# Attention layer of a four-layer graph network: halves of x prepared one step earlier, projections and aggregation in another order, a shorter softmax chain

## The reference

```python
def _L1_gnn_ref(x, adj_matrix, W_qk, W_v):
    qk = jnp.einsum('bnd,ed->bne', x, W_qk)
    q, k = jnp.split(qk, 2, axis=-1)
    v = jnp.einsum('bnd,ed->bne', x, W_v)
    inv_scale = 1.0 / ATT_DIM ** 0.5
    scores = jnp.einsum('bnd,bmd->bnm', q, k) * inv_scale
    w = jnp.sum(scores * adj_matrix, axis=-1, keepdims=True)
    w = jax.nn.softmax(w, axis=1)
    return w * v
...
x = _layernorm(x + _L0_gnn_ref(x, adj, ...), axis=-1)
x = _layernorm(x + _L1_gnn_ref(x, adj, L1_gnn_W_qk, L1_gnn_W_v), axis=-1)
x = _layernorm(x + _L2_gnn_ref(x, adj, ...), axis=-1)
x = _layernorm(x + _L3_gnn_ref(x, adj, ...), axis=-1)
```

## Time and profile before

| | |
|---|---|
| median of 3 runs | 685.64 us (684.79 to 686.12) |
| the profiled execution | 688.34 us, of which the span of its trace is 686.5 us |
| granted PE clock over the span | 0.982 |
| PE busy | 630.0 us (92%), DVE 563.2 us (82%), ACT 528.3 us (77%), POOL 372.0 us (54%) |
| layer 1 on PE | from 284.4 us to 390.6 us of the span |

### The profile page before, as it was taken

How to read it: one execution, slowest core, us unless ns; L and a number is a source line. 1 busy time by engine, 2 the same in 40 slices (tenths; PEclk the granted TensorE clock), 3 DMA queues, 4 the chain that set the end, 5 groups by cost and what they waited for, 6 DMA issues and landing times.

```text
span 686.5 us, 15919 instructions
## 1 busy us (share of the span) xinstructions
PE 630.0 (92%) x5014; PEld 454.4 (66%) x5014; DVE 563.2 (82%) x1744; ACT 528.3 (77%) x1191; POOL 372.0 (54%) x448
## 2 busy tenths in 40 slices
PE   5899999999999999789999789999999997999993
PEld 4577777777777776556655456676767564778782
DVE  3899988888888886768887859898989897578886
ACT  4667888777777887668887776787778785799995
POOL 1335556665555555756665524444444343798883
PEclk9999999999999999999999899999999998999998
DMA  9682439364554322566665523645444443487883
GB/s 278 180 210 52 91 70 224 80 160 94 142 120 97 63 32 47 107 134 130 139 136 111 93 63 77 100 90 105 91 95 94 98 88 63 79 179 182 175 189 124
DMA packets 176771, 80.35 MB, mean 117 GB/s; under 512 B 122416, under 2 KB 174128, under 8 KB 176688
## 3 DMA queue, kind: packets, MB, share of 16 engines
q1 hardware_dynamic: 166512, 70.54, 43.7%
q0 software_dynamic: 8448, 8.39, 8.4%
q10 hardware_dynamic: 1728, 0.40, 0.3%
HBM read 28.97 MB, written 8.39 MB: 54 GB/s over the span
## 4 chain that ended last, share of the span: by engine, by line
PE 31%; DMA 8%; DVE 7%; POOL 7%; issue 4%; ACT 3%; SPq 0%; ACTq 0%; POOLq 0%; DVEq 0%
PE banks L86 10%; PE banks L88 9%; PE banks L87 9%; DMA xT_lo<-x_halves 6%; POOL x_halves L1130 3%; DMA l_TT_lo<-l_T_lo 2%; DVE l_st L1044 2%; POOL l_rstd L1069 2%; DVE l_pre L1321 1%; POOL l_U L1976 1%; PE banks L1569 1%; PE banks L1847 1%; ACT x_resident L1078 1%; POOL l_T_lo L1773 1%; PE banks L1234 1%
## 5 line engine op out<-in xcount | busy, mean ns | idle before, releaser
L1078 ACT ACTIVATE x_resident<-l_pre,l_nmr,l_rstd 128x256 f32<-128x256 f32 x256 | 142.1, 606 | 10.6 <-POOL l_nmr L1072 9.9
L973 POOL TENSOR_TENSOR hq<-hq 128x512 f32<-128x512 f32 x48 | 69.4, 1446 | 94.1 <-ACT hq L690 91.8
L1130 POOL TENSOR_TENSOR x_halves<-x_resident,x_halves 128x1024 f16<-128x1024 f32 x46 | 98.1, 2132 | 28.5 <-DVE l_pre L1321 24.4
L1044 DVE BATCH_NORM_STATS2 l_st<-l_pre 128x6 f32<-128x256 f32 x256 | 92.2, 412 | 0.0
L86 PE MATMUL banks<-Wk_lo,xT_hi 128*128 128x258 f16 (+1 forms) x256 | 84.3, 329 | 1.2 <-DVE l_hr L1691 0.6
L87 PE MATMUL banks<-Wk_hi,xT_lo 128*128 128x258 f16 (+1 forms) x256 | 84.2, 329 | 0.0
L88 PE MATMUL banks<-Wk_hi,xT_hi 128*128 128x258 f16 (+1 forms) x256 | 84.1, 329 | 0.0
L1069 POOL TENSOR_TENSOR l_rstd<-l_veps,minus_half 128x4 f32<-128x4 f32 x64 | 70.1, 1095 | 18.5 <-DVE l_veps L1058 14.2
L86 PE MATMUL banks<-W2T_lo,h_hi 128*128 128x257 f16 x256 | 70.3, 274 | 5.2 <-ACT zf L702 3.4
L88 PE MATMUL banks<-W2T_hi,h_hi 128*128 128x257 f16 x256 | 70.1, 274 | 0.0
L87 PE MATMUL banks<-W2T_hi,h_lo 128*128 128x257 f16 x256 | 70.1, 274 | 0.0
(11 more groups left out here) (202 smaller groups left out, 1911.0 us busy)
## 6 DMA issues: line engine op xcount, KB each, us to landing
adj<-in_adj SPq DMA_DIRECT2D x32, 256.0 KB, 3.7
x_halves<-in_x SPq DMA_DIRECT2D x16, 512.0 KB, 4.4
x_resident<-b_half SPq DMA_DIRECT2D x8, 1024.0 KB, 8.1
x_resident<-in_x POOLq DMA_DIRECT2D x16, 512.0 KB, 6.0
out<-x_resident SPq DMA_DIRECT2D x15, 512.0 KB, 3.3
l_adjT<-adjT_resident SPq DMA_DIRECT2D x16, 256.0 KB, 2.6
x_resident<-in_L_gnn_W SPq DMA_DIRECT2D x2, 512.0 KB, 5.4
x_resident<-in_L_gnn_Wk SPq DMA_DIRECT2D x1, 768.0 KB, 9.6
```

What stands on the lines that cost most here:

```text
L973: pool.tensor_tensor(hq[:, 0, :], hq[:, 0, :], hq[:, h, :], ALU.add).then_inc(hqs_ok, 1)
L1044: dve.bn_stats(L.st[p][:, j, :], L.pre[p][:, j, :]).then_inc(L.st_ok, 1)
L1078: act.activation(K.x[:, gcols(g, j)], L.pre[p][:, j, :], ACT.Identity, bias=L.nmr[p][:, j:j + 1], scale=L.rstd[p][:, j:j + 1]).then_inc(L. ...
L1130: pool.tensor_tensor(F.xs[p][1], x_group(K, g), F.xs[p][0], ALU.subtract).then_inc(F.x_lo, 1)
```

## The change

In layer 1:

- The halves of x for group g+3, not g+2, are made and transposed in step g of ACT, POOL and SP; ACT makes the high half ahead of all four `norm_apply`, not behind the first.
- `aggregate` reads the resident adjacency itself; the copies `l_adjT` and their 16 DMAs are gone.
- PE's step is now project(g-1, 3), weight_columns(g-2), project(g, 0), aggregate(g-1), project(g, 1), the first half of project(g, 2), score_rows(g-1), the second half of project(g, 2).
- The factor -SC goes into the product with q, so that DVE's minimum of the rows is at once the bias of the exponential; the separate negation is gone.
- `residual` takes the weights as its per-partition scalar straight from PSUM; their copy to SBUF is gone.
- DVE's order: two rows of statistics, the minimum, the other two rows, the division (softmax), and then the variance.
- SP's seam between layers 0 and 1 is 'noonnn', not 'nononn'.

```diff
-SEAMS_SP = ('nononn', 'oono', 'onooonon')
+SEAMS_SP = ('noonnn', 'oono', 'onooonon')
...
-            if halves_due(F, g + 2):
-                transpose_x(F, sp, g + 2, p, (qkv_ps, GP))
-            if has(2):
-                stage_adj(g + 2, p)
+            if halves_due(F, g + 3):
+                transpose_x(F, sp, g + 3, 1 - p, (qkv_ps, GP))
...
         def aggregate(g, p):
-            pe.wait_ge(a_in[p], 8 * (g - p) + 16)
             pe.wait_ge(qkv_sb, upto(g, GP, GP))
...
-                m = pe.matmul(b_as[p][:, j * (QK + 1):(j + 1) * (QK + 1)], ast[p][:, j * N:(j + 1) * N],
+                m = pe.matmul(b_as[p][:, j * (QK + 1):(j + 1) * (QK + 1)],
+                              K.at[:, g * C + j * N:g * C + (j + 1) * N],
                               vqk[p][:, j, D + QK:D + 2 * QK + 1], start=True, stop=True)
...
                 weight_columns(g - 2, p)
+            if has(0):
+                project(g, p, 0)
             if has(-1):
                 aggregate(g - 1, q)
             if has(0):
-                project(g, p, 0)
                 project(g, p, 1)
+                project(g, p, 2, 0)
             if has(-1):
                 score_rows(g - 1, q)
             if has(0):
-                project(g, p, 2)
+                project(g, p, 2, 1)
...
-            act.activation(wexp[p][:], b_as[p][0:GP, rows], ACT.Exp, bias=wneg[p][:], scale=SC,
+            act.activation(wexp[p][:], b_as[p][0:GP, rows], ACT.Exp, bias=wmin[p][:], scale=-1.0,
                            accum_out=wsum[p][:]).then_inc(wexp_ok, 1)
...
+            if halves_due(F, g + 3):
+                high_half(g + 3, q)
             if has(-2):
                 norm_apply(K, L, act, g - 2, p, 0)
-            if halves_due(F, g + 2):
-                high_half(g + 2, p)
-            if has(-2):
                 norm_apply(K, L, act, g - 2, p, 1)
...
-            dve.tensor_copy(wgt[p][:], b_as[p][:, cols]).then_inc(wgt_ok, 1)
...
-            dve.scalar_tensor_tensor(L.pre[p][:, j, :], vqk[p][:, j, 0:D], wgt[p][:, j:j + 1],
+            dve.scalar_tensor_tensor(L.pre[p][:, j, :], vqk[p][:, j, 0:D], b_as[p][:, cols.start + j:cols.start + j + 1],
                                      K.x[:, gcols(g, j)], ALU.mult, ALU.add).then_inc(L.pre_ok, 1)
...
-            dve.tensor_tensor(qa[:], ak[:, :, 0:QK], vqk[p][:, :, D:D + QK], ALU.mult).then_inc(qa_ok, 1)
+            dve.scalar_tensor_tensor(qa[:], ak[:, :, 0:QK], -SC, vqk[p][:, :, D:D + QK], ALU.mult,
+                                     ALU.mult).then_inc(qa_ok, 1)
...
-            dve.tensor_reduce(wmax[p][:], b_as[p][0:GP, rows], AX.X, ALU.max).then_inc(wmax_ok, 1)
-            dve.wait_ge(wmax_ok, upto(g, 1, 1))
             if reused(g):
                 dve.wait_ge(wexp_ok, upto(g - 2, 1, 1))
-            dve.tensor_scalar(wneg[p][:], wmax[p][:], -SC, None, ALU.mult).then_inc(wneg_ok, 1)
+            dve.tensor_reduce(wmin[p][:], b_as[p][0:GP, rows], AX.X, ALU.min).then_inc(wmin_ok, 1)
...
                 norm_row(L, dve, g - 2, p, 1)
+            if has(-1):
+                minimum(g - 1, q)
+            if has(-2):
                 norm_row(L, dve, g - 2, p, 2)
                 norm_row(L, dve, g - 2, p, 3)
-            if has(-1):
-                maximum(g - 1, q)
             once(g, 0, ones, 1)
+            if has(-1):
+                softmax(g - 1, q)
             if has(-2):
                 norm_variance(L, dve, g - 2, p, EPS)
-            if has(-1):
-                softmax(g - 1, q)
-                weights(g - 1, q)
...
         def low_half(g, p):
-            if reused(g, 3):
-                pool.wait_ge(L.pre_ok, upto(g - 3, GP, GP))
+            if reused(g, 4):
+                pool.wait_ge(L.pre_ok, upto(g - 4, GP, GP))
...
-            if halves_due(F, g + 2):
-                low_half(g + 2, p)
+            if halves_due(F, g + 3):
+                low_half(g + 3, 1 - p)
```

More of the change, by code:

```diff
@@ L1160, in layer1 @@
     vqk = [sb("vqk0", [128, GP, D + 2 * QK + 1])]
-    ast = [sb(f"adjT{p}", [128, C]) for p in range(2)]
     qa = sb("qa", [128, GP, QK])
@@ L1165, in two @@
         return [sb(f"{name}{p}", shape) for p in range(2)]
-    w, wexp, wn, wgt = two("w", [128, GP]), two("wexp", [GP, N]), two("wn", [GP, N]), two("wgt", [128, GP])
-    wmax, wneg, wsum, wrec = (two(name, [GP, 1]) for name in ("wmax", "wneg", "wsum", "wrec"))
+    w, wexp, wn = two("w", [128, GP]), two("wexp", [GP, N]), two("wn", [GP, N])
+    wmin, wsum, wrec = (two(name, [GP, 1]) for name in ("wmin", "wsum", "wrec"))
     vqk.append(sb("vqk1", [128, GP, D + 2 * QK + 1]))
@@ L1172, in layer1 @@
     qkv_ps, qkv_sb, k_one, ak_ps = map(sem, ("qkv_ps", "qkv_sb", "k_one", "ak_ps"))
[L1173 to L1176, removed]
+    qa_ok, w_ok, asum_ok, wT_ps, wmin_ok, wexp_ok, wrec_ok, wn_ok, wB_ps = map(
+        sem, ("qa_ok", "w_ok", "asum_ok", "wT_ps", "wmin_ok", "wexp_ok", "wrec_ok", "wn_ok", "wB_ps"))
     SC = 1.0 / (W_SCALE * W_SCALE * QK ** 0.5)
     F = front_of(K.F, 1)
-    K.qkv_sb, K.asum_ok, K.qa_ok, K.wgt_ok = qkv_sb, asum_ok, qa_ok, wgt_ok
+    K.qkv_sb, K.asum_ok, K.qa_ok, K.weighted = qkv_sb, asum_ok, qa_ok, L.pre_ok
     K.x_new[1], K.scores_after[2] = L.x_new, []
     def sync(sp):
[L1184 to L1192, removed]
         def step(g, p, has):
-            if halves_due(F, g + 2):
-                transpose_x(F, sp, g + 2, p, (qkv_ps, GP))
-            if has(2):
-                stage_adj(g + 2, p)
+            if halves_due(F, g + 3):
+                transpose_x(F, sp, g + 3, 1 - p, (qkv_ps, GP))
             if is_first(g):
@@ L1205, in tensor, with project @@
     def tensor(pe):
-        def project(g, p, j):
+        def project(g, p, j, half=None):
             if j == 0:
                 transposed(F, pe, g, p)
-            if reused(g, 1):
+            if half == 1:
+                pass
+            elif reused(g, 1):
                 pe.wait_ge(qkv_sb, upto(g - 1, GP, j + 1))
@@ L1216, in project @@
             for d in range(DT):
-                m = triple(nc, b_qkv[j][:, 0:2 * QK + D], [s[:, j, d, :] for s in F.xT[p]],
-                           [w[:, d, :] for w in K.qkv], start=d == 0, stop=d == DT - 1)
-            m.then_inc(qkv_ps, 1)
+                if half is None or d == half:
+                    m = triple(nc, b_qkv[j][:, 0:2 * QK + D], [s[:, j, d, :] for s in F.xT[p]],
+                               [w[:, d, :] for w in K.qkv], start=d == 0, stop=d == DT - 1)
+            if half != 0:
+                m.then_inc(qkv_ps, 1)
         def aggregate(g, p):
-            pe.wait_ge(a_in[p], 8 * (g - p) + 16)
             pe.wait_ge(qkv_sb, upto(g, GP, GP))
@@ L1225, in aggregate @@
                 pe.wait_ge(k_one, 2)
+                pe.wait_ge(free["copied"], G)
             if reused(g):
@@ L1228, in aggregate @@
                 pe.wait_ge(qa_ok, upto(g - 2, 1, 1))
+                pe.wait_ge(L.pre_ok, upto(g - 2, GP, GP))
             else:
```

19 lines of the change are left out of this document (7 added, 12 removed).

## The result

The median of six executions is 681.31 us (679.51 to 684.61) against 685.72 (684.79 to 687.36, six executions) for the kernel before on the same chip. The ratio is 0.9924, 95% interval 0.9901 to 0.9946: 4.4 us faster. The forecast was 679.2 us, range 675.5 to 683.5.

A forecast was written before the change was run, and what follows sets the result against it. PE was taken to bound layer 1. Against the profiled 688.34 us: 0.8 - 5.0 - 2.7 - 0.9 = -7.8; with half the slow step counted, -6.4 on the median 685.64, 679.2 us, range 675.5 to 683.5.

The forecast's parts named there:

- Steady step: Layer 1, one weight_columns to the next: 5.52 us forecast, against 5.94 on average before, counted for 12 steps.
- the slow step: Layer 1's one step of 8.25 us, PE waiting for a transposed low half; forecast to become 5.52, saving 2.73 us.
- the forecast's first rival: Softmax chain or ACT binds instead of PE: step 5.8 us, gain 3.0, time 682.6 us; chance 0.18.
- What is late next: Variance behind division: scales ready 1.86 us after weight_columns starts; ACT waits some 0.2 us, leaving 0.26 of the step.
- Weights from PSUM: DVE's residual without the copy starts 0.20 us earlier, hidden by its wait for aggregate; PSUM scalar costs 0 per instruction.
- Softmax chain: From score_rows to weight_columns, two of four statistics inside: 1.78 us, against PE's 1.72, so PE waits 0.06.
- Halves a step ahead: Transposed low half lands 1.2 us before PE wants it; such waits and the lower clock after them go, 2.73 us.
- Start: Layer 1's start: aggregate(1) now behind project(2, 0) adds 0.92, less 0.15 for lighter transpose traffic; 0.8 us later.
- End: Layer 1's last chain: division 0.67 us earlier, missing weights copy 0.20; together 0.9 us earlier.
- Total: Sum against the profiled execution -7.8 us, 680.5; on the median, half the slow-step gain counted, -6.4, 679.2 us.
- the third rival: Late transposed low half stalls PE's project(g, 0), 2.7 us per such step; slower from three, 691.4 us with four; chance 0.08.
- the forecast's signs of being wrong: Weight_columns to weight_columns above 5.8 us, mid-layer waits on xT_lo, or other layers moving by more than 1.5 us.

## Why the prediction was right, and where it was off

- **Steady step**: forecast 5.52, measured 5.54 on average; with the slow step 7.7 us forecast, 7.43 measured. The size was right, the reason partly not. The hole closed further (0.31, not 0.38) and PE's own step is 5.27 to 5.31, not 5.46. What kept the step at 5.54 was the ring through the scales, the forecast's first rival in mechanism if not in price. That the shorter step of PE and the wait of 0.24 add up to the forecast is luck. And the gain was put down to PE's order, 0.31 a step, where that order gave 0.15 and DVE's, variance behind division, 0.34 (4.43 over 13 steps); the two were taken out singly and need not add up.
- **What is late next**: the term that was mis-sized. Scales were put at W + 1.86 and came at W + 2.17 (339.49 less 337.32); 0.28 of the 0.31 is the reciprocal root beside residual, 1.29 against 1.01. ACT's wait of "some 0.2" was 0.72, which used up the 0.26 kept in reserve. And the forecast counted ACT's load, not its place in a closed ring with the division: a ring needs no full engine to bind.
- **Weights from PSUM**: nothing per instruction, as taken. But the 0.20 by which residual moves was costed on DVE alone, where it is hidden; it fell on POOL. This is the step that failed in kind: "In the steady step DVE then waits for aggregate anyway".
- **Softmax chain**: S to W 1.78 forecast, 1.97 measured, 0.24 of it the wait for the ring. With the ring shortened, S to W holds no wait, so the chain by itself fits.
- **Halves a step ahead**: no wait after group 2, as forecast, and without it 14 us more. Half of one slow step was counted for the median; the runs cannot say how many such steps the other executions of before had.
- **Start**: forecast 0.8, measured 1.71. The half landed 0.36 later than before (4.04 us from issue to use, not 3.44 less 0.15); why is open, see the last section. And from project(2, 0) to W(1) it was 7.14 us against 5.79, 0.43 more than the 0.92 of aggregate. This last is the lower clock, which the longer idle time (3.55 us) did not shorten: once PE ran again it was at the lower level for 4.5 us (to 306.9), against 3.4 (299.4 to 302.8) before. W(1), forecast near 305.6, was at 309.50, or 306.55 with layer 0's 2.95 taken off.
- **End**: 0.9 forecast. 0.61 is seen in W(14) to W(15); the other 0.2 to 0.3 lies behind W(15), within the spread of the later layers, and is not shown.
- **Total**: -6.65 us in the profiled executions after layer 0's 2.95 is taken off, against -7.8. On the medians -4.4 against -6.4. As an estimate from these numbers, the profiled execution of before without its slow step (688.34 - 2.73 = 685.6) and that of after without its slow start (684.61 - 2.95 = 681.7) both come out at their medians. That fits a median of before without the slow step; then the half of it that the forecast counted, 1.4 us, is most of the 2.0 missing. It is not shown.
- **Two slips in the text**: in the third rival two slow steps (5.4 us) outweigh the 5.0, not only three. And one of the forecast's signs of being wrong, another layer moving by more than 1.5 us, did show in the profiled execution: layer 0, by 2.95. I don't count it against the change, since half of the kernels show it and their layer 0 on PE is the same.

**Still open**: why layer 0 starts slowly in some executions. Six of twelve profiled kernels had their layer 1 start at 286 to 288 us, the others at 283.5 to 284.4. There is one profiled execution of each, so it isn't known whether the kernel or the execution decides; that other executions of the changed kernel were up to 5.1 us shorter than the profiled one (679.51 against 684.61) speaks for the execution.

## What to carry to other kernels

When an instruction moves behind another, follow its result round until it comes back to the same engine; a ring of waits over three engines bound this step though no engine in it was full. In the kernel before, such a ring of PE and DVE bound it, and closing a hole in PE's queue alone gained nothing. Cost an edit also by whom the neighbours now meet: a removed copy of 0.16 us made the step 0.2 longer. And where all of a pipeline's stages are deepened by one step, look at its first round by itself: here it cost 5.5 us, and another place in the seam for one operation of POOL gave them back.
